# Two feed-forwards in an audio tower: a down projection that runs two inner blocks behind gate and up, and rows that are split into fp16 halves before they are transposed

## Chip, cores, metric

One core of one Trainium2 chip. The metric is the time of one execution on the device in microseconds, the median of several runs. The profile is of one further execution.

## What is computed

Four layers on 4096 rows of 512: an attention-like token mixer, an attention, a feed-forward with ternary weights, an attention with linear bias and a feed-forward with fp4 weights. The change touches the two feed-forwards:

```python
h = h + _L0_ffn_ref(_layernorm(h, axis=-1), L0_ffn_w1, L0_ffn_w3, L0_ffn_w2)
h = h + _L1_attn_ref(_layernorm(h, axis=-1), L1_attn_Wq, L1_attn_Wk, L1_attn_Wv, L1_attn_Wo)
h = h + _L1_ffn_ref(_layernorm(h, axis=-1), L1_ffn_gate_up_packed, L1_ffn_gate_up_scales, L1_ffn_down_packed, L1_ffn_down_scales)
...
g = jax.nn.silu(h1) * h3                                  # first: h1, h3 = x @ ternary w1, w3
return jnp.einsum('bsh,dh->bsd', g, w2q)
...
w_gu = _dequant_fp4(gate_up_packed, gate_up_scales, GROUP_SIZE)   # second: one scale per 128 inputs
h = jax.nn.silu(gate) * up
y = jnp.einsum('bsi,hi->bsh', h, w_down)
rms = jnp.sqrt(jnp.mean(y * y, axis=-1, keepdims=True) + EPS)
return y / rms
```

The inner width is 1365 in the first and 1408 in the second: 11 inner blocks of up to 128.

## The kernel before

The instructions of each engine are written out by hand in the order in which it runs them; semaphores order the engines among each other. Both feed-forwards work in 8 groups of 512 rows, each of 4 tiles of 128 rows. A step `n` runs the 11 inner blocks `m` of group `n`; beside them stand the down projection of group `n-1` and the normalisation of the tiles of group `n+1`, at the blocks in `norm_at` (3, 5, 7, 9).

**Rows.** A tile is normalised on VectorE (`row_stats`, `x_normalised`, with an inverse root on GpSimd between them) into the fp32 tile xn. TensorE transposes xn in four fp32 pieces into the bank px (`transpose_x`, L1728 in the first, L2129 in the second). ScalarE casts px to fp16 (xhi), VectorE subtracts that from px (xlo). The next xn waits for the transposes, the next transposes for xlo. Every product is made with both halves.

**First feed-forward** (`feed_forward`, from L1464). For each inner block TensorE makes 16 matmuls of 512 columns (gate_up, L1717), at blocks 2, 4, 6, 8 also 22 matmuls that project one tile of the group before (finish, L1740), and at 3, 5, 7, 9 a tile's transposes. ScalarE makes silu, VectorE the product prod and glo, ScalarE ghi. In groups 1 to 7 three of five blocks also hold a slot of the decode of the fp4 weights: masks and a join on VectorE (L1394 to L1409), four activations and a cast on ScalarE (L1432 to L1445), two or three products and sums on GpSimd (`pool_value`, L1454 to L1461), loads on SP. GpSimd runs `pool_value` of a block ahead of its inverse root.

**Second feed-forward** (`feed_forward_fp4`, from L1759). As the weights have a scale for each 128 inputs, a block's gate and up are 8 separate sums of two matmuls each (`products_of`, L2119). They go round six banks part0 to part5. ScalarE scales every second one into a tile (`scale_part`, L1922), VectorE scales and adds the ones between (`join_part`, L2006), GpSimd adds the two tiles (`sum_parts`, L1888). The projection of group `n-1` is spread over all 22 half blocks by the table `down_to`, tile after tile, into one bank pz, 33 matmuls each (`project`, L2141); ScalarE copies pz out before the next tile begins (`z_out`, L1954):

```python
down_to = {0: (0, 0, 6), 1: (0, 6, 12), 2: (0, 12, 18), 3: (0, 18, 23), 4: (0, 23, 28), 5: (0, 28, 33),
           6: (1, 0, 7), 7: (1, 7, 14), 8: (1, 14, 21), 9: (1, 21, 27), 10: (1, 27, 33),
```

Then come squares (L1962), mean square (L2054), inverse root (L1875), hout (`output`, L2063) and the store. The last step, `n` = 8, has no gate and up: it projects group 7 alone.

**Between the two** lies the second attention. Its last steps alternate with `normalise(i)` of the second feed-forward's first four tiles, on each engine in its own order (L2160 and on). On VectorE `normalise(i)` is xn, statistics of the next tile, xlo; then the next attention step begins with hout (L837).

## Time and profile before

| | |
|---|---|
| Median of 3 runs | 2389.77 us (2387.38 to 2393.89) |
| Profiled execution, its own time | 2391.57 us |
| Its span | 2389.8 us |
| TensorE busy, share of the span | 2244.2 us, 94% |
| VectorE | 1662.7 us, 70% |
| ScalarE | 1495.3 us, 63% |
| GpSimd | 1021.4 us, 43% |
| Granted TensorE clock | 0.985 |
| Token mixer and first attention | 0 to 957 us |
| First feed-forward, second attention, second feed-forward | 957 to about 1470, to 1801, to 2389.8 us |

Busy time of TensorE is the time in which at least one matmul is under way. Matmuls are pipelined, so a matmul of 512 columns is shown with 0.38 us though the next starts sooner; the distance of starts tells what one costs. Names of tiles stand without their number, f_ is either feed-forward, a_ either attention, fw_ the fp4 decode.

### The profile page before, as it was taken

To read this page: it belongs to the slowest core of one execution; us is meant where nothing else is said; L and a number is where in the kernel's file an instruction comes from. 1 tells how busy PE (TensorE), PEld (TensorE's weight loads), DVE (VectorE), ACT (ScalarE), POOL (GpSimd) and SP (SyncE) were. 2 spreads that over 40 slices of the span, in tenths; PEclk is the share of its full clock that TensorE was granted. 3 is DMA by queue.
4 is the path that set the end of the run, shared out by engine and by line. 5 is a ranking of instruction groups with operands and counts; after the bars stand their busy time and mean duration, and the time that the engine had idled before them with its cause. 6 is when DMAs were issued, how large, how long until landed. Compare 5 with 4: busy or idle time off the path is not lost. (4 is left out here: it accounts for less than half of the span.)

```text
span 2389.8 us, 41107 instructions
## 1 busy us (share of the span) xinstructions
PE 2244.2 (94%) x13188; PEld 1128.5 (47%) x13188; DVE 1662.7 (70%) x2931; ACT 1495.3 (63%) x2398; POOL 1021.4 (43%) x1007
## 2 busy tenths in 40 slices
PE   6999999998999996799999999999987999999998
PEld 2333333335666663344444445666652444444443
DVE  6666666665888887456667634666657888888873
ACT  4666666666788785355656425667745666667663
POOL 1222222237777773223324302444434555555552
PEclk9999999999999998799999999999999999999999
DMA  5545445442343211312223212222221011111101
GB/s 146 138 127 135 129 127 135 130 110 66 111 131 114 67 58 36 109 50 79 80 89 93 67 48 84 80 79 79 79 67 40 23 49 40 53 41 45 45 27 53
DMA packets 144300, 194.94 MB, mean 82 GB/s; under 512 B 32773, under 2 KB 76261, under 8 KB 144154
## 3 DMA queue, kind: packets, MB, share of 16 engines
q1 hardware_dynamic: 115642, 154.79, 21.7%
q10 hardware_dynamic: 28512, 38.28, 5.7%
q8 instruction: 81, 1.33, 0.2%
q14 instruction: 65, 0.53, 0.1%
HBM read 125.10 MB, written 42.21 MB: 70 GB/s over the span
## 5 line engine op out<-in xcount | busy, mean ns | idle before, releaser
L341 DVE TENSOR_REDUCE tm_negmax<-tm_s 128x1 f32<-128x512 f32 x512 | 323.3, 679 | 164.7 <-PE tm_s L384 164.4
L303 ACT ACTIVATE tm_prob<-tm_s 128x1024 f32<-128x1024 f32 x256 | 257.6, 1023 | 136.9 <-PE tm_s L404 130.6
L2119 PE MATMUL f_part<-f_xhi,gu 128*128 128x512 f16 x704 | 269.4, 383 | 17.8 <-ACT f_firstg L1922 6.3
L2119 PE MATMUL f_part<-f_xlo,gu 128*128 128x512 f16 x704 | 268.6, 382 | 0.0
L421 PE MATMUL tm_o<-tm_prob,tm_vt 128*64 128x512 f32 x1024 | 255.7, 620 | 0.0
L1888 POOL TENSOR_TENSOR f_firstg<-f_firstg,f_secondg 128x512 f32<-128x512 f32 x88 | 150.7, 1712 | 193.3 <-DVE f_secondg L2006 193.3
L2141 PE MATMUL f_pz<-dn,f_ghi 128*128 128x512 f16 x704 | 214.5, 380 | 5.9 <-ACT f_zc L1954 5.9
L384 PE MATMUL tm_s<-tm_qk 96*128 96x512 f16 x512 | 199.2, 391 | 14.6 <-DMA tm_qk<-tm_xs 14.1
L264 POOL TENSOR_TENSOR tm_hn<-tm_nd,tm_rows 128x1024 f32<-128x1024 f32 x32 | 75.3, 2353 | 291.8 <-DMA tm_rows<-rden 291.8
L404 PE MATMUL tm_s<-tm_qk 98*128 98x512 f16 x512 | 194.2, 382 | 1.6 <-DMA tm_qk<-tm_mrow 1.6
L975 PE MATMUL a_bankB<-a_wo,a_yThi 128*128 128x512 f16 x512 | 158.7, 393 | 4.1 <-DVE a_yTlo L899 4.0
L1015 PE MATMUL a_bankB<-a_wqkv,a_xhi 128*128 128x512 f16 x512 | 152.9, 380 | 0.3
L1888 POOL TENSOR_TENSOR f_firstu<-f_firstu,f_secondu 128x512 f32<-128x512 f32 x88 | 117.9, 1339 | 70.2 <-DVE f_secondu L2006 69.4
L421 PEld LDWEIGHTS tm_o<-tm_prob,tm_vt 128*64 128x64 f32 x1024 | 92.4, 199 | 112.2 <-issue 85.7
L1740 PE MATMUL f_pz<-tern,f_ghi 128*128 128x512 f16 (+1 forms) x352 | 134.3, 382 | 2.9 <-DVE f_glo L1641 2.9
L1740 PE MATMUL f_pz<-tern,f_glo 128*128 128x512 f16 (+1 forms) x352 | 134.1, 381 | 0.0
L2141 PE MATMUL f_pz<-dn,f_glo 128*128 128x512 f16 x352 | 133.4, 379 | 0.0
L2119 PEld LDWEIGHTS f_part<-f_xhi,gu 128*128 128x128 f16 x704 | 69.1, 98 | 122.4 <-ACT f_firstg L1922 14.1
L384 PEld LDWEIGHTS tm_s<-tm_qk 96*128 96x128 f16 x512 | 50.0, 98 | 155.4 <-issue 86.9
L1456 POOL TENSOR_TENSOR fw_value<-fw_value,fw_code 128x512 f32<-128x512 f32 (+1 forms) x35 | 43.9, 1254 | 185.0 <-DVE fw_value L1409 178.1
L683 ACT COPY a_qT<-a_bankD 128x512 f16<-128x512 f16 x128 | 68.6, 588 | 83.4 <-PE a_bankD L948 83.4
L694 ACT COPY a_kT<-a_bankC 32x512 f16<-32x512 f16 (+1 forms) x192 | 111.1, 578 | 1.5
(190 smaller groups left out, 5668.4 us busy)
## 6 DMA issues: line engine op xcount, KB each, us to landing
tm_qk<-tm_xs SPq DMA_DIRECT2D x384, 64.0 KB, 2.1
tm_xqk<-in_qk ACTq DMA_DIRECT2D x32, 512.0 KB, 4.3
a_hin<-h SPq DMA_DIRECT2D x64, 256.0 KB, 2.7
a_hres<-h SPq DMA_DIRECT2D x64, 256.0 KB, 3.0
h<-a_hout SPq DMA_DIRECT2D x64, 256.0 KB, 2.5
f_hin<-h SPq DMA_DIRECT2D x64, 256.0 KB, 2.7
f_hres<-h SPq DMA_DIRECT2D x64, 256.0 KB, 2.8
tm_vt<-in_vt ACTq DMA_DIRECT2D x32, 256.0 KB, 3.0
```

What stands on the lines that cost most here:

```text
L303: nc.scalar.activation(prob[b][:, 2 * h:2 * h + 2, :], s2[:, i % 2, :, :], ACT.Exp, scale=SCALE).then_inc(exp_done, 1)
L341: nc.vector.tensor_reduce(negmax[u][:, m:m + 1], s1[:, p % BANKS, :], AX.X, ALU.max, negate=True).then_inc(s1_read, 1)
L384: nc.tensor.matmul(s1[:, place(m) % BANKS, :], qk[u][0:KS, 0, b, i * P:(i + 1) * P], qk[u][0:KS, 1, b, :], start=True, stop=True).then_inc ...
L404: last = nc.tensor.matmul(s2[:, i % 2, j, :], qk[u][0:KM, 1, b, s:s + P], qk[u][0:KM, 0, b, :], start=True, stop=True)
L421: last = nc.tensor.matmul(o[2 * C * q:2 * C * (q + 1), :], vt[u][:, j, :, b], prob[b][:, j, :], start=j == 0, stop=j == NT - 1)
L694: last = nc.scalar.copy(kT[rows, :, :, :, j, :].rearrange("p a f b k -> p (a f b) k"), kTp[rows, :].rearrange("p (n k) -> p n k", k=L))
L975: last = nc.tensor.matmul(bankB[:, :], a, w[:, r, :], start=n == 0, stop=n == 3 * R - 1)
L1015: last = nc.tensor.matmul(out, a[u][:, j, :], w[:, j, cols], start=n == 0, stop=n == 3 * KT - 1)
L1740: last = nc.tensor.matmul(pz[i % 2][:, :], gparts[x][u][0:rows[m], m, i * P:(i + 1) * P], down[0:rows[m], m, :], start=c == 0, stop=c == 2 ...
L1888: pool.tensor_tensor(to[:, :], to[:, :], other[:, :], ALU.add).then_inc(s["sum_done"], 1)
L2119: last = nc.tensor.matmul(part[q % BANKS][:, :], (gate, up)[which][:, j, m * P:(m + 1) * P], xparts[x][u][:, j, :], start=x == 0, stop=x == 1)
L2141: last = nc.tensor.matmul(pz[:, :], gparts[x][u][:, m, i * P:(i + 1) * P], down[w][:, m, :], start=c == 0, stop=c == 3 * MT - 1)
```

## The change

**Both feed-forwards.** xn is no longer transposed in fp32. ScalarE casts it to fp16 into halves[:, 0] (`x_high`), GpSimd subtracts that from xn into halves[:, 1] (`x_low`), TensorE transposes both halves in eight fp16 pieces into one bank, and ScalarE copies all 1024 columns to xs (`copy_x`), one block later. VectorE's xlo is gone. The next xn waits for `x_low`, the next split for the transposes, the next transposes for the copy.

**Second feed-forward.** Four banks hold the sums of the four tiles at once, four others take gate and up in turn, with the transposes as one more user of the turn. The projection of block `m-2` runs beside gate and up of block `m`: 12 matmuls, one or two after each pair. The projection of a group so ends two blocks after its gate and up, in the next step. The copies of the sums come in blocks 1 and 2, squares, means and outputs in blocks 3 to 10 of that step. The last step has 24 matmuls. Product and glo of a group's last block moved into block 0 of the next step.

```diff
 def feed_forward(...):
+        def x_low(g, i):
+            if inside(g, GROUPS):
+                t = NT * g + i
+                wait(pool, s["high_done"], t + 1)
+                wait(pool, s["xT_ready"], t)
+                pool.tensor_tensor(halves[:, 1, :], xn[:, :], halves[:, 0, :], ALU.subtract).then_inc(s["low_done"], 1)
...
                 if q is not None:
                     fp4.pool_value(pool, q - 1)
+                if m + 1 in norm_at:
+                    x_low(n + 1, norm_at.index(m + 1))
                 if m + 3 in norm_at:
                     inverse_deviation(n + 1, norm_at.index(m + 3))
...
+        def x_high(g, i):
+            if inside(g, GROUPS):
+                t = NT * g + i
+                wait(act, s["xn_done"], t + 1)
+                wait(act, s["xT_ready"], t)
+                nc.scalar.copy(halves[:, 0, :], xn[:, :]).then_inc(s["high_done"], 1)
+        def copy_x(g, i, u):
             if inside(g, GROUPS):
                 wait(act, s["xT_ready"], NT * g + i + 1)
                 if i == 0:
                     wait(act, s["gu_ready"], MT * (g - 1))
+                nc.scalar.copy(xs[u][:, :, :, i * P:(i + 1) * P].rearrange("p x j n -> p (x j) n"),
+                               px[:, :].rearrange("p (n c) -> p n c", c=P)).then_inc(s["xs_done"], 1)
...
             for m in range(MT):
                 q = slot(n, m)
+                if m - 1 in norm_at:
+                    copy_x(n + 1, norm_at.index(m - 1), 1 - u)
+                if m + 1 in norm_at:
+                    x_high(n + 1, norm_at.index(m + 1))
                 gate_act(n, m, u)
                 if m:
                     hidden_hi(n, m - 1, u)
                 if q is not None:
                     fp4.scalar_high(act, q - 3)
-                if m in norm_at:
-                    x_hi(n + 1, norm_at.index(m), 1 - u)
...
-        def x_lo(g, i, u):
-            if inside(g, GROUPS):
-                wait(dve, s["xhi_done"], NT * g + i + 1)
-                nc.vector.tensor_tensor(xlo[u][:, :, i * P:(i + 1) * P], px[:, :].rearrange("p (j n) -> p j n", j=KT),
-                                        xhi[u][:, :, i * P:(i + 1) * P], ALU.subtract).then_inc(s["xlo_done"], 1)
...
 def feed_forward_fp4(...):
+    turn = [bank[i] for i in (3, 4, 5, 2)]
+    pz = [bank[i] for i in (6, 7, 0, 1)]
...
+    squares_at = [3, 5, 7, 8]
+    mean_at = [4, 6, 8, 9]
+    out_at = [5, 7, 9, 10]
+    LAG = 2
...
+        def step(n):
             for m in range(MT):
+                lagging = (n, m - LAG) if m >= LAG else (n - 1, MT + m - LAG)
                 for which in range(2):
                     for j in range(KT):
-                        products_of(n, m, u, which, j)
-                    project(n - 1, 1 - u, *down_to[2 * m + which])
+                        i = 4 * which + j
+                        products_of(n, m, which, j)
+                        for c in range(3 * i // 2, 3 * (i + 1) // 2):
+                            project(*lagging, c)
                 if m in norm_at:
                     transpose_x(n + 1, norm_at.index(m))
...
 sync:
+            store(n - 1, 0)
             residual(n - 1, 2)
             load(n + 2, 0)
             store(n - 1, 1)
             residual(n - 1, 3)
             load(n + 2, 1)
+            store(n - 1, 2)
+            store(n - 1, 3)
...
 scalar, normalise(i) of the first four tiles:
-            x_hi(0, i, 0)
+            if i:
+                copy_x(0, i - 1, 0)
+            if i < NT:
+                x_high(0, i)
```

GpSimd in group 1 of the first feed-forward, blocks 0 to 5, before (f_rstd is the inverse root, fw_value the two fp4 operations of one chunk):

```order
L1570 TENSOR_TENSOR f_rstd_10644<-f_veps_10642,f_minus_half 128x1
L1456 TENSOR_TENSOR fw_value_10626<-fw_value_10626,fw_code_10622 128x512
L1461 TENSOR_TENSOR fw_value_10626<-fw_value_10626,fw_words_10616 128x512
L1570 TENSOR_TENSOR f_rstd_10645<-f_veps_10643,f_minus_half 128x1
L1456 TENSOR_TENSOR fw_value_10627<-fw_value_10627,fw_code_10623 128x512
L1461 TENSOR_TENSOR fw_value_10627<-fw_value_10627,fw_words_10617 128x512
L1570 TENSOR_TENSOR f_rstd_10644<-f_veps_10642,f_minus_half 128x1
```

The same place of the changed kernel:

```order
L1578 TENSOR_TENSOR f_rstd_10644<-f_veps_10642,f_minus_half 128x1
L1456 TENSOR_TENSOR fw_value_10626<-fw_value_10626,fw_code_10622 128x512
L1461 TENSOR_TENSOR fw_value_10626<-fw_value_10626,fw_words_10616 128x512
L1573 TENSOR_TENSOR f_halves<-f_xn,f_halves 128x512
L1578 TENSOR_TENSOR f_rstd_10645<-f_veps_10643,f_minus_half 128x1
L1456 TENSOR_TENSOR fw_value_10627<-fw_value_10627,fw_code_10623 128x512
L1461 TENSOR_TENSOR fw_value_10627<-fw_value_10627,fw_words_10617 128x512
L1573 TENSOR_TENSOR f_halves<-f_xn,f_halves 128x512
```

The subtraction that the transposes of the next block wait for stands behind the chunk's two fp4 operations.

TensorE at the last gate and up products of the second feed-forward and behind them, before (f_part is a bank of a gate or up sum, f_pz the bank of the down projection; 138 projections follow the last product, 6 of them in its own half block):

```order
L2119 MATMUL f_part<-f_xhi_10730,gu 128x512
L2119 MATMUL f_part<-f_xlo_10732,gu 128x512
L2141 MATMUL f_pz<-dn_10611,f_ghi_10737 128x512
L2141 MATMUL f_pz<-dn_10612,f_ghi_10737 128x512
L2141 MATMUL f_pz<-dn_10611,f_glo_10739 128x512
L2141 MATMUL f_pz<-dn_10611,f_ghi_10737 128x512
L2141 MATMUL f_pz<-dn_10612,f_ghi_10737 128x512
L2141 MATMUL f_pz<-dn_10611,f_glo_10739 128x512
```

The same place of the changed kernel (all banks are named f_bank):

```order
L2171 MATMUL f_bank<-dn_10611,f_ghi_10736 128x512
L2143 MATMUL f_bank<-f_xs_10730,gu 128x512 x2
L2171 MATMUL f_bank<-dn_10612,f_ghi_10736 128x512
L2171 MATMUL f_bank<-dn_10611,f_glo_10738 128x512
L2171 MATMUL f_bank<-dn_10611,f_ghi_10736 128x512
L2171 MATMUL f_bank<-dn_10612,f_ghi_10736 128x512
L2171 MATMUL f_bank<-dn_10611,f_glo_10738 128x512
L2171 MATMUL f_bank<-dn_10611,f_ghi_10736 128x512
```

The projection is mixed among the products, and 26 projections are left behind the last of them.

VectorE where a tile of the second feed-forward is normalised between two steps of the attention, before (a_hout is the attention's output, f_xlo the low half) and in the changed kernel:

```order
L2042 TENSOR_SCALAR f_xn<-f_hin_10715,f_mv_10723,f_rstd_10727 128x512
L2030 BN_STATS f_stats_10720<-f_hin_10714 128x6
L2032 BN_AGGR f_mv_10722<-f_stats_10720 128x2
L2034 TENSOR_SCALAR f_veps_10724<-f_mv_10722 128x1
L2048 TENSOR_TENSOR f_xlo_10731<-f_px,f_xhi_10729 128x4x128
L837 TENSOR_TENSOR a_hout_10675<-a_bankB,a_hres_10673 128x512
```

```order
L2098 TENSOR_SCALAR f_xn<-f_hin_10713,f_mv_10721,f_rstd_10725 128x512
L2086 BN_STATS f_stats_10720<-f_hin_10714 128x6
L2088 BN_AGGR f_mv_10722<-f_stats_10720 128x2
L2090 TENSOR_SCALAR f_veps_10724<-f_mv_10722 128x1
L837 TENSOR_TENSOR a_hout_10675<-a_bankB,a_hres_10673 128x512
```

The operation that waited for TensorE's transposes is gone from ahead of a_hout.

## Rows read from the trace of the kernel before

**Rows 1.** Windows: length, busy PE, PEld, DVE, ACT, POOL (count); clock, DMA, GB/s.

```profile
977.40:1437.00 459.60, 452.71 (x2136) 213.67 (x2136) 274.92 (x464) 230.75 (x382) 130.20 (x114) 0.99 0.24 76
1801.00:1862.00 61.00, 48.76 (x193) 15.73 (x194) 50.46 (x83) 41.25 (x69) 32.76 (x25) 0.97 0.09 27
1862.00:2349.80 487.80, 480.66 (x2247) 219.88 (x2248) 407.10 (x636) 337.91 (x568) 262.43 (x206) 1.00 0.13 41
2349.80:2389.80 40.00, 30.44 (x138) 12.98 (x136) 8.03 (x15) 8.06 (x18) 4.36 (x7) 0.98 0.19 66
```

**Rows 2.** Chain that ended last: start us, us, what.

```profile
2301.74 1.73 PE f_part L2119 x8
```

**Rows 3.** Timeline of PE: transposes in fp32 and in fp16. Start us, us, what.

```profile
1820.99 0.60 PE L2129 MATMUL f_px<-f_ident,f_xn 128*128 128x128 f32 x4
...
1509.48 0.61 PE L948 MATMUL a_bankD<-a_ident,a_qs 128*128 128x128 f16 x8
```

**Rows 4.** Timeline of PE: second feed-forward, first and third inner block.

```profile
1800.96 0.59 PE L2119 MATMUL f_part<-f_xhi,gu 128*128 128x512 f16 x1 [1.49 <-DVE f_xlo L2048]
...
1811.41 0.39 PE L2119 MATMUL f_part<-f_xhi,gu 128*128 128x512 f16 x1 [0.22 <-DVE f_secondg L2006]
```

**Rows 5.** Timelines of ACT and DVE: the last tile.

```profile
2383.08 0.59 ACT L1954 COPY f_zc<-f_pz 128x512 f32<-128x512 f32 x1 [6.63 <-PE f_pz L2141]
2383.70 0.63 ACT L1962 ACTIVATE f_square<-f_zc 128x512 f32<-128x512 f32 x1
...
2385.27 0.75 DVE L2063 SCALAR_TENSOR_TENSOR f_hout<-f_zc,f_rinv,f_hres 128x512 f32<-128x512 f32 x1 [0.66 <-POOL f_rinv L1875]
```

**Rows 6.** DMA issues on the page: KB, us to landing.

```profile
f_hres<-h SPq DMA_DIRECT2D x64, 256.0 KB, 2.8
```

**Rows 7.** Groups by line: busy us, mean ns, idle before.

```profile
L1888 POOL TENSOR_TENSOR f_firstg<-f_firstg,f_secondg 128x512 f32<-128x512 f32 x88 | 150.7, 1712 | 193.3 <-DVE f_secondg L2006 193.3
L2006 DVE SCALAR_TENSOR_TENSOR f_firstg<-f_part,f_factor,f_firstg 128x512 f32<-128x512 f32 x88 | 65.8, 748 | 24.6 <-ACT f_firstg L1922 18.0 <-PE f_part L2119 6.2
L1922 ACT ACTIVATE f_firstg<-f_part,f_factor 128x512 f32<-128x512 f32 x88 | 60.4, 687 | 14.1 <-PE f_part L2119 14.1
```

**Rows 8.** Timelines of PE and DVE: drain of the second attention.

```profile
1774.70 0.60 PE L2129 MATMUL f_px<-f_ident,f_xn 128*128 128x128 f32 x4
...
1775.95 0.69 DVE L2048 TENSOR_TENSOR f_xlo<-f_px,f_xhi 128x512 f16<-128x512 f32 x1 [3.42 <-ACT f_xhi L1945]
1776.56 0.68 DVE L837 TENSOR_TENSOR a_hout<-a_bankB,a_hres 128x512 f32<-128x512 f32 x1
```

**Rows 9.** Timelines of DVE and PE: opening of the first feed-forward.

```profile
965.34 0.55 DVE L1661 TENSOR_SCALAR f_xn<-f_hin,f_mv,f_rstd 128x512 f32<-128x512 f32 x1 [0.73 <-POOL f_rstd L1570]
968.38 0.54 DVE L1661 TENSOR_SCALAR f_xn<-f_hin,f_mv,f_rstd 128x512 f32<-128x512 f32 x1
...
977.44 0.61 PE L1717 MATMUL f_gu0g<-f_xhi,tern 128*128 128x512 f16 x1 [1.40 <-DVE f_xlo L1667]
```

**Rows 10.** Timeline of ACT: 1024 elements out of a bank.

```profile
933.51 1.01 ACT L733 CAST a_pThi<-a_bankS 128x1024 f16<-128x1024 f32 x1 [1.58 <-PE a_bankS L1024]
```

**Rows 11.** Timelines of POOL, PE, ACT, DVE: two tiles of the first feed-forward.

```profile
1036.24 1.26 POOL L1461 TENSOR_TENSOR fw_value<-fw_value,fw_words 128x512 f32<-128x512 f32 x1
...
1038.42 0.60 PE L1728 MATMUL f_px<-f_ident,f_xn 128*128 128x128 f32 x4
...
1333.85 0.68 ACT L1590 ACTIVATE f_act_out<-f_gu0g,tern_scales 128x512 f32<-128x512 f32 x1
...
1337.74 0.54 DVE L1661 TENSOR_SCALAR f_xn<-f_hin,f_mv,f_rstd 128x512 f32<-128x512 f32 x1
...
1342.97 1.54 POOL L1461 TENSOR_TENSOR fw_value<-fw_value,fw_words 128x512 f32<-128x512 f32 x1
...
1339.92 0.60 PE L1728 MATMUL f_px<-f_ident,f_xn 128*128 128x128 f32 x4
```

**Rows 12.** Groups by line: gate products of odd blocks.

```profile
L1717 PE MATMUL f_gu1g<-f_xhi,tern 128*128 128x512 f16 (+1 forms) x176 | 66.7, 379 | 2.9 <-DVE f_xlo L1667 2.9
```

More of the change, by code:

```diff
@@ L2055, in mean_square, with output @@
                     .then_inc(s["ms_done"], 1)
-        def output(g, i, half):
+        def output(g, i):
             if inside(g, GROUPS):
@@ L2087, in step, with products_of @@
+                join_part(n, m, 1, 3)
+                if m in out_at:
+                    output(n - 1, out_at.index(m))
                 if m + 3 in norm_at:
-                    i = norm_at.index(m + 3)
-                    row_stats(n + 1, i, 2 * (n + 1) + i // 2)
-            hidden(n, MT - 1, u)
-            hidden_lo(n, MT - 1, u)
+                    row_stats(n + 1, norm_at.index(m + 3))
         return normalise, begin, step
     def tensor(pe):
+        def products_of(g, m, which, j):
+            if inside(g, GROUPS):
+                i = 4 * which + j
+                if m == 0 and i == 0:
+                    wait(pe, s["xs_done"], NT * (g + 1))
+                wait_bank(pe, g, m, i)
+                for x in range(2):
+                    last = nc.tensor.matmul(bank_of(m, i)[:, :], (gate, up)[which][:, j, m * P:(m + 1) * P],
+                                            xs[g % 2][:, x, j, :], start=x == 0, stop=x == 1)
+                last.then_inc(s["part_ready"], 1)
@@ new lines, in transpose_x @@
+        def transpose_x(g, i):
+            if inside(g, GROUPS):
+                t = NT * g + i
+                px = (bank_of(None, i) if g else turn[3])[:, :].bitcast(F16)
+                wait(pe, s["low_done"], t + 1)
+                if g:
+                    wait_bank(pe, g - 1, None, i)
+                else:
+                    wait(pe, s["xs_done"], t)
+                for x in range(2):
+                    for j in range(KT):
+                        last = nc.tensor.transpose(px[:, (x * KT + j) * P:(x * KT + j + 1) * P],
+                                                   halves[:, x, j * P:(j + 1) * P], ident[:, :])
+                last.then_inc(s["xT_ready"], 1)
@@ new lines, in project @@
+        def project(g, m, c):
+            if inside(g, GROUPS):
+                i, (x, w) = c // 3, products[c % 3]
+                if c == 0:
+                    wait(pe, s["glo_done"], MT * g + m + 1)
+                if m == 0 and c % 3 == 0:
+                    wait(pe, *(pz_free[i] if g == 0 else (s["zc_done"], NT * (g - 1) + i + 1)))
+                last = nc.tensor.matmul(pz[i][:, :], gparts[x][g % 2][:, m, i * P:(i + 1) * P], down[w][:, m, :],
+                                        start=m == 0 and c % 3 == 0, stop=m == MT - 1 and c % 3 == 2)
+                if m == MT - 1 and c % 3 == 2:
+                    last.then_inc(s["z_ready"], 1)
@@ L2100, in begin @@
         def begin():
-            for n in ("qT_copied", "pTlo_done", "y_done", "yTlo_done"):
+            for n in ("qT_copied", "pTlo_done"):
                 pe.wait_ge(*before.done[n])
-        def sums_begin():
-            pe.wait_ge(*before.done["out_done"])
-        def products_of(g, m, u, which, j):
-            if inside(g, GROUPS):
-                i = 4 * which + j
-                q = 8 * m + i
-                if q == 0:
-                    wait(pe, s["xlo_done"], NT * (g + 1))
-                used = 8 * MT * g + q - BANKS if q >= BANKS else 8 * MT * (g - 1) + (84 if q < 4 else 78) + q
-                if q >= BANKS or not isinstance(g, int) or g:
-                    wait(pe, s[("scale_done", "join_done")[j % 2]], used // 2 + 1)
-                for x in range(2):
-                    last = nc.tensor.matmul(part[q % BANKS][:, :], (gate, up)[which][:, j, m * P:(m + 1) * P],
-                                            xparts[x][u][:, j, :], start=x == 0, stop=x == 1)
-                last.then_inc(s["part_ready"], 1)
@@ L2195, in _ @@
         att.all_rows(sp)
-        run(step_u, 0, 9)
+        for n in range(9):
+            step_u(n)
         unit_rows(sp)
@@ L2219, in _ @@
             normalise(i)
-        run(step_u, 0, 9)
+        for n in range(9):
+            step_u(n)
     @block.scalar
@@ L2247, in _ @@
                 run(step, 31 + i, 31 + i)
-        run(step_u, 0, 9)
+        normalise(4)
+        for n in range(9):
+            step_u(n)
     @block.vector
@@ L2273, in _ @@
         begin()
-        run(step_u, 0, 9)
+        for n in range(9):
+            step_u(n)
     @block.tensor
@@ L2295, in _ @@
         begin()
-        run(step_u, 0, 0)
-        sums_begin()
-        run(step_u, 1, 9)
+        for n in range(9):
+            step_u(n)
 def three_bf16(a):
```

290 lines of the change are left out of this document (138 added, 152 removed), and 3 rows, old and new, of the table down_to.

## The prediction

> **What bounds the kernel now.** I read the page's busy shares first and then the busy time in windows [rows 1]. In the first feed-forward TensorE is busy for 452.7 of 459.6 us, in groups 1 to 7 of the second for 480.7 of 487.8 us. Two stretches of the second are different: its group 0 (61.0 us, 48.8 busy) has nothing to project yet, and in the last 40.0 us there is only projection left. So TensorE's stream of matmuls sets the time nearly everywhere, and whatever makes it wait is paid in full. The yardstick is the chain of waits [rows 2]: eight 512-column matmuls start within 1.73 us, 0.216 us each.
>
> **Transposes.** Four fp32 ones take 0.60 us from the first start to the last end, eight fp16 ones 0.61 us [rows 3]. TensorE wins nothing from halves: cost 0 for all 64 tiles, and the change must live from the order of work.
>
> **Second feed-forward, groups 1 to 7.** 7 x (176 + 132) matmuls x 0.216 = 465.7 us, and six sets of four tiles' transposes at 0.43 us (0.60 less the 0.17 us by which a matmul outlasts its turn) = 10.3 us: 476.0 us if nothing waits, against 487.8 and the 1.3 us of six projections of the last block that ran behind the window's end, 489.1. The waits that go are those of the single sum pz (it had to be copied out between two tiles) and of the burst at a group's end. Can four banks carry it? An inner block is now 28 matmuls, 6.05 us; a bank comes round after four pairs and their share of projection, 3.0 us. ScalarE has per block four scalings and some copies, VectorE four joins (means 0.69 and 0.75 us [rows 7]) and two passes of the hidden values: about 3.9 us each, and up to 5.9 us where norms and outputs fall too. Laid end to end on the 6.05 us, the bank needed soonest is free 1.0 us early or more. I take -13.1 us; bounds 0 (as many waits as before) and -14 us.
>
> **Group 0.** The third inner block started 10.4 us after the first [rows 4]. With four banks instead of six to fill ahead I take 11.4. From there the projection of block 0 runs along: 9 x 6.05 + 4 x 0.43 = 56.2. Group 0 takes 67.6 instead of 61.0: +6.6 us (bounds +5 to +9).
>
> **The end.** After the last block there were 132 matmuls and the chain of the last tile, 38.7 us (40.0 less those 1.3). Now there are 24 matmuls. The last glo needs one sum on GpSimd, the product, ghi and glo: ready about 3.9 us after the last products, so TensorE waits 1.4 us and ends at 6.6. The four tiles are then ready together, and their chains queue: four copies at 0.59 on ScalarE, four squares at 0.8 with the read of their sums [rows 5], so output 1 is done at 10.6. The third and fourth output need residuals that SP loads only after outputs 0 and 1, 2.8 us to landing [rows 6]: output 3 starts at 13.9. From the last hout's start to the end of the span it was 4.5 us [rows 5]. That makes 18.4 us where it was 38.7: -20.3 us (bounds -17 and -22).
>
> **Attention's drain.** VectorE stood at xlo, which needs the transposes, and those were queued behind 12 matmuls of the output projection; only after xlo came hout and the next tile's work [rows 8]: hout started 1776.56, while its own bank was complete about 1775.0. xlo is gone, so hout moves up 1.6 us in two rounds: -3.2. The last tile's chain is longer (ScalarE split, GpSimd subtraction, 1.01 us copy [rows 10] instead of 0.59 + 0.69), but its normalisation starts earlier: about 0. Bounds 0 and -3.3. Second feed-forward in all: -13.1 + 6.6 - 20.3 - 3.2 = **-30.0 us**.
>
> **First feed-forward, the opening.** Before, one tile took 3.0 us (xn 965.34, 968.38) and the first product started at 977.44 [rows 9]. Now a tile's ring is split on ScalarE 0.6, subtraction on GpSimd 1.3, transposes 1.1 at the low clock, copy of 1024 elements 1.0 [rows 10], since one pair of halves and one bank serve all: 4.1 us. +5.0 us for four tiles (4 to 6).
>
> **First feed-forward, the tiles on the way.** This is the largest unknown. GpSimd runs the fp4 decode; the new subtraction stands behind the two fp4 sums of its inner block, and those wait for a VectorE join that itself comes after this block's product. TensorE reaches the transposes 38 matmuls, 8.2 us, after the gate and up sums of that block. Laying 1.27 us (an fp4 product takes 1.26 and 1.54 in [rows 11]) plus 0.1 us behind GpSimd's end for each of the 28 tiles of groups 0 to 6, 17 are in time and 11 are late, by 16.2 us in sum. The first late one: GpSimd free at 1037.5, subtraction to 1038.9, transposes had started 1038.42. The worst: GpSimd free at 1344.5, transposes at 1339.92 [rows 11]. A second pass counts what the new ScalarE work adds ahead of silu (it must now wait for xn, and where the decode ran just before, the copy of the previous tile stands there too): in group 6 silu ran at 1333.85, xn ends 1338.28, so product, join and fp4 sums all move by 1.5 us, and that tile is 7.5 us late. Eight others move by 0.6 to 1.7 us; waits already paid take some away. I get **22.5 us**. Bounds: 10 (half absorbed by later slack) and 28. Two of these waits are over 3.5 us. After the drain and its last wait of 1.49 us [rows 4], group 0 of the second part ran at a granted clock of 0.97 over 61 us [rows 1], 1.8 us lost; two of that: +3.6 (0 to 7).
>
> **First feed-forward, group borders.** At three borders TensorE waited 2.9 us for xlo (f_gu1g [rows 12]; two more at f_gu0g). Now the copy of the last tile stands behind four decode steps of ScalarE in the same block: 1.5 us more, three times, +4.5 (2 to 6). All: 5.0 + 22.5 + 3.6 + 4.5 = **+35.6 us**.
>
> Hidden and costed at nothing: split and 1.01 us copy in the second part (ScalarE was busy 338 of 488 us, the change adds some 4 us a group), x_low there (GpSimd 262 of 488), xlo's removal from VectorE (407 of 488). If that cover were gone, 0.5 us a tile, 14 us.
>
> **The sum.** 2391.57 us is the profiled execution's own time. 2391.6 - 30.0 + 35.6 = 2397.2. That execution lies 1.8 us above the median of 2389.77, so the forecast for the median is **2395 us**: two large terms of opposite sign that nearly cancel. A measurement of this kernel can tell about 0.3% (7 us) from no change, so this is "the same", at its upper edge.
>
> **Rivals.**
> - *The late tiles of the first part are absorbed* (0.25). For it: 17 of 28 tiles had 0.3 to 5.5 us of slack, and every wait of TensorE gives the other engines time to catch up, also at the borders. Against: the chain starts from the same gate and up sums each time, so a wait doesn't shorten the next one. If only the opening and 8 us are left, 2389.8 - 30 + 13 = 2373 us.
> - *Four banks are too few* (0.10): slower, the other side. If one bank in each inner block comes free 0.35 us late (a join behind a late hout would do it), TensorE loses 0.35 x 77 = 27 us and the time is 2422 us. It decides once VectorE or ScalarE needs more than about 1 us above what I laid end to end. The six banks of before still waited in the first blocks of a group, and so it isn't excluded.
> - *The subtraction on GpSimd is longer* (0.20). The same form on GpSimd takes 1.26 us at its shortest [rows 11] but 1.71 in the mean beside VectorE's joins [rows 7]. With 1.75 in place of 1.27, 11 to 14 tiles are 0.5 us later, and VectorE operations held up move joins too: 7 to 13 us more, 2405 us. The Trainium skill (SBUF — State Buffer, "Who interferes with whom") says that a VectorE instruction with two SBUF inputs and a GpSimd instruction that reads SBUF exclude each other for a whole instruction; the 1.71 beside 1.27 agrees, and by that rule this rival is the likelier of the two slower ones.
> - That the change doesn't do what it says I leave out: the order on TensorE shows two gate and up products between projections of one block down to the end.
>
> **Numbers.** Forecast 0.45 with a range of its own of 2387 to 2403: 0.03 faster, 0.32 within 0.3%, 0.10 slower. Absorbed 0.25: 0.22 and 0.03. Four banks 0.10: slower. Longer subtraction 0.20: 0.05 within and 0.15 slower. Together: faster 0.25, same 0.40, slower 0.35. The range that leaves out 2 in 10 reaches into the first rival below and past the third above: 2372 to 2413 us.
>
> **What would show it.** Right, if group 0 of the second part lasts 66 to 69 us, each later group 68 to 68.5, and the stretch after the last gate product 17 to 20; if TensorE waits for the new GpSimd subtraction some 15 to 25 us between the first and last transposes of the first part, the longest in its group 6; and if the first gate product comes about 5 us later. Wrong, if gate and up products wait for scalings or joins in every block (four banks), or if the first part is longer by under 15 us.

## The result, and the profile after

The changed kernel takes **2400.31 us** (median of 9 runs, 2396.65 to 2402.76); the kernel before, timed beside it, 2391.58 us (9 runs, 2386.39 to 2395.74). The ratio is 1.0035, 95% interval 1.0023 to 1.0046: 8.7 us slower, clear of no change; the 0.3% (7 us) that the forecast took as the edge of "the same" lies inside the interval, so on which side of that edge the kernel stands isn't settled (a chance of 0.35 stood on slower, 0.40 on the same). The time is inside the range of 2372 to 2413 us. The profiled execution took 2401.46 us with a span of 2399.7 us. All times below are medians, and each stands beside the kernel before as timed with it on the same chip; of the run `residuals_early` one of four executions (3632 us, at a clock of 0.60) was disturbed and isn't used.

First, the busy time in windows of the changed kernel, cut at the same events as in [rows 1]: first feed-forward, group 0 and groups 1 to 7 of the second, and what follows the last gate and up product (length, then busy PE, PEld, DVE, ACT, POOL with counts; clock, DMA share, GB/s).

```profile
985.80:1478.10 492.30, 462.53 (x2248) 215.47 (x2248) 269.90 (x436) 258.59 (x410) 161.71 (x142) 0.97 0.22 71
1836.40:1903.60 67.20, 65.64 (x316) 29.40 (x317) 50.25 (x80) 47.90 (x74) 37.69 (x29) 0.97 0.08 24
1903.60:2379.30 475.70, 475.70 (x2348) 221.54 (x2347) 376.75 (x613) 359.02 (x594) 295.63 (x230) 1.00 0.13 42
2379.30:2399.70 20.40, 5.89 (x27) 2.31 (x25) 6.15 (x12) 6.48 (x15) 3.94 (x6) 0.75 0.34 116
```

In groups 1 to 7 TensorE is now busy without a gap: 475.70 of 475.70 us. The first feed-forward grew from 459.6 to 492.3 us, and of the 32.7 us more only 9.8 are busy time.

TensorE's waits in the first feed-forward, by what ended them (engine, line, releaser: us in total, times, longest):

```profile
PE f_px L1740 <- POOL f_halves L1573: 19.9, 7, 7.4
PE f_gu1g L1728 <- ACT f_xs L1622: 5.3, 2, 2.7
PE f_gu0g L1728 <- DVE f_prod L1653: 3.0, 3, 1.5
PE f_gu0g L1728 <- ACT f_xs L1622: 2.4, 2, 1.3
```

The first row is new: seven sets of transposes wait for GpSimd's subtraction. Counted from start to start it is 21.4 us, since a matmul's shown end lies 0.17 us behind its turn and an eighth wait of 0.3 us is too short for the list. The worst of them on GpSimd's timeline (start us, us, what, idle time and releaser) ...

```profile
1375.20 1.27 POOL L1456 TENSOR_TENSOR fw_value<-fw_value,fw_code 128x512 f32<-128x512 f32 x1 [5.63 <-DVE fw_value L1409]
1376.61 1.53 POOL L1461 TENSOR_TENSOR fw_value<-fw_value,fw_words 128x512 f32<-128x512 f32 x1
1378.11 1.60 POOL L1573 TENSOR_TENSOR f_halves<-f_xn,f_halves 128x512 f16<-128x512 f32 x1
```

... and what TensorE, ScalarE and VectorE did meanwhile:

```profile
1370.49 1.89 PE L1728 MATMUL f_gu1u<-f_xs,tern 128*128 128x512 f16 x8
1379.77 1.04 PE L1740 MATMUL f_px<-f_ident,f_halves 128*128 128x128 f16 x8 [7.39 <-POOL f_halves L1573]
...
1370.60 0.62 ACT L1615 CAST f_halves<-f_xn 128x512 f16<-128x512 f32 x1 [4.53 <-DVE f_xn L1680]
1371.12 0.68 ACT L1600 ACTIVATE f_act_out<-f_gu0g,tern_scales 128x512 f32<-128x512 f32 x1
...
1374.44 0.68 DVE L1409 TENSOR_TENSOR fw_value<-fw_value,fw_bend 128x512 f32<-128x512 f32 x1
```

The high half was there at 1371.2. GpSimd stood still for 5.63 us before the fp4 sum, waiting for VectorE's join (ready at 1375.1), while the subtraction behind it had all it needed. The join was late for the same kind of reason one engine further on: on ScalarE the silu of the next product (1371.12) now stands behind the cast, and the cast waited 4.53 us for xn. Against the moment at which TensorE came to its transposes, the join ended 2.9 us late here (1375.1 against 1372.2) and 1.5 us late at the same tile before (1341.5 against 1339.9 [rows 11]), as VectorE's row there shows:

```profile
1340.78 0.68 DVE L1409 TENSOR_TENSOR fw_value<-fw_value,fw_bend 128x512 f32<-128x512 f32 x1
```

What remains after the last gate and up product, on VectorE, TensorE, GpSimd, ScalarE and SP's queue, to compare with [rows 5, 6]:

```profile
2379.59 0.75 DVE L2062 SCALAR_TENSOR_TENSOR f_secondu<-f_bank,f_factor,f_secondu 128x512 f32<-128x512 f32 x1 [0.64 <-ACT f_secondu L1970]
2380.42 1.71 POOL L1934 TENSOR_TENSOR f_firstu<-f_firstu,f_secondu 128x512 f32<-128x512 f32 x1 [1.05 <-DVE f_secondu L2062]
...
2383.59 0.69 DVE L2078 TENSOR_TENSOR f_glo<-f_prod,f_ghi 128x512 f16<-128x512 f32 x1 [0.68 <-ACT f_ghi L1986]
2384.34 0.60 PE L2171 MATMUL f_bank<-dn,f_ghi 128*128 128x512 f16 x2 [1.91 <-DVE f_glo L2078]
2385.20 2.53 ACT L2010 COPY f_zc<-f_bank 128x512 f32<-128x512 f32 x4 [1.64 <-PE f_bank L2171]
2387.62 0.63 ACT L2018 ACTIVATE f_square<-f_zc 128x512 f32<-128x512 f32 x1
...
2391.84 0.43 SPq L1860 DMA_DIRECT2D f_hres<-h  x1
2395.13 0.75 DVE L2113 SCALAR_TENSOR_TENSOR f_hout<-f_zc,f_rinv,f_hres 128x512 f32<-128x512 f32 x1 [1.02 <-DMA f_hres<-h]
```

The glo that TensorE waits for is ready at 2384.3, 5.3 us after the last product started (2379.0), and before the last output VectorE idles 1.02 us for a residual that was issued at 2391.84.

### The profile page after: what moved, and what is told of

Same layout as the page of the kernel before. It is cut to its first block and busy times, and to the rows that moved or that the text cites. A ratio compares the mean times of both kernels' runs of the same rounds, so it can differ in the third digit from the quotient of the medians.

```text
span 2399.7 us, 41805 instructions
## 1 busy us (share of the span) xinstructions
PE 2241.7 (93%) x13444; PEld 1136.8 (47%) x13444; DVE 1621.3 (68%) x2867; ACT 1557.2 (65%) x2462; POOL 1100.0 (46%) x1071
## 5 line engine op out<-in xcount | busy, mean ns | idle before, releaser
L2143 PE MATMUL f_bank<-f_xs,gu 128*128 128x512 f16 x1408 | 418.6, 380 | 2.8 <-ACT f_xs L2001 1.2
L2171 PE MATMUL f_bank<-dn,f_ghi 128*128 128x512 f16 x704 | 265.5, 379 | 1.9 <-DVE f_glo L2078 1.9
L2143 PEld LDWEIGHTS f_bank<-f_xs,gu 128*128 128x128 f16 x1408 | 136.4, 98 | 164.9 <-issue 3.7
L1934 POOL TENSOR_TENSOR f_firstu<-f_firstu,f_secondu 128x512 f32<-128x512 f32 x88 | 124.0, 1409 | 65.0 <-DVE f_secondu L2062 65.0
L2171 PE MATMUL f_bank<-dn,f_glo 128*128 128x512 f16 x352 | 133.4, 379 | 0.0
L635 POOL TENSOR_TENSOR a_qs<-a_qkv,a_qs 128x512 f16<-128x512 f32 x32 | 37.1, 1159 | 173.7 <-ACT a_qs L752 173.7
L611 POOL TENSOR_TENSOR a_crossed<-a_qkv,a_sin 128x64 f32<-128x64 f32 (+1 forms) x128 | 81.7, 657 | 76.4 <-ACT a_qkv L722 76.3
```

Source lines behind the costliest of these rows:

```text
L611: pool.tensor_tensor(dst[:, :, :, e], src[:, :, :, 1 - e], sin[:, e, :].unsqueeze(1).broadcast_to([P, n, 8]), ALU.mult).then_inc(s["crosse ...
L1934: pool.tensor_tensor(to[:, :], to[:, :], other[:, :], ALU.add).then_inc(s["sum_done"], 1)
L2143: last = nc.tensor.matmul(bank_of(m, i)[:, :], (gate, up)[which][:, j, m * P:(m + 1) * P], xs[g % 2][:, x, j, :], start=x == 0, stop=x == 1)
L2171: last = nc.tensor.matmul(pz[i][:, :], gparts[x][g % 2][:, m, i * P:(i + 1) * P], down[w][:, m, :], start=m == 0 and c % 3 == 0, stop=m == ...
```

## Experiments

**Each part alone.** `second_only` is the changed kernel with the first feed-forward of before, whole, and a second, fp16 identity beside the fp32 one; `first_only` the reverse. Beside the exchanged function the edit is this:

```diff
+    ident16 = sb("ident16", [P, P], F16)
+        sp.dma_start(ident16[:, :], const["ident16"]).then_inc(c_in, 16)
```

> Only the second feed-forward is changed; the first keeps fp32 transposes and the old xhi/xlo. Theory (the terms are independent and each as it stands in the trace of the change: attention's stretch -5.8 us, groups of the second part -5.8, end -19.7): 31 us less than before, 2360 us (2355 to 2365). Rival A (the two parts are coupled: part of the second part's gain is time that was only shifted there by the later start of its inputs): 2365 to 2375. Also looked at: in the changed kernel TensorE had a half-clock stretch at 562 to 580 us, in code that neither part touches, worth 4 us; if it came from where code or tiles lie, this kernel shows it too, if it is chance, it may not.

> Only the first feed-forward is changed; the second keeps the old order and the old xhi/xlo. Theory (opening 4.2 us, waits for halves at the transposes 21.4, borders 3.0, clock after the waits 6 to 9): 35 to 38 us more than before, about 2427 us. Rival (the waits are partly absorbed by attention behind it, where the stretch became 5.8 us shorter in the changed kernel): 2415 to 2422 us.

Measured: second part alone 2364.15 us against 2394.93, ratio 0.9877 [0.986, 0.9893], **-30.8 us**; first part alone 2432.26 against the same, 1.0163 [1.0146, 1.018], **+37.3 us**. The sum, +6.5, is within 2.2 us of what both together cost (+8.7), less than the intervals of some 4 us can tell from nothing. The stages say it more sharply: groups 1 to 7 of the second part last 475.4 us with either first part. No interaction is seen, and rival A of the first and the rival of the second fall. From first to last gate and up product the first feed-forward lasts 491.7 us in `first_only` and 492.3 in the changed kernel, 459.4 in `second_only` and before.

**The subtraction ahead of the fp4 sums.** In the changed kernel, first part:

```diff
+                if m + 1 in norm_at:
+                    x_low(n + 1, norm_at.index(m + 1))
                 if q is not None:
                     fp4.pool_value(pool, q - 1)
-                if m + 1 in norm_at:
-                    x_low(n + 1, norm_at.index(m + 1))
```

> The changed kernel, with the GpSimd subtraction of the first part ahead of the fp4 sums of its inner block instead of behind them. Theory (the transposes wait only because the subtraction stands behind the fp4 sums, and the half-clock stretches come from those waits): the 21.4 us of waits fall under 3, the stretches at half clock inside groups 1 to 6 of the first part go, 26 to 30 us less than the changed kernel: 2370 to 2374 us. Rival A (the split on ScalarE, which waits for xn, is late itself): waits of 8 to 12 us stay, 2382 to 2388. Rival B (the fp4 sums move 1.2 us later and ScalarE's or VectorE's decode steps with them, so silu and the product are late): TensorE waits for the product instead, gate and up sums start late by 0.5 to 1 us in 28 blocks, 2385 to 2400.

Measured: 2375.96 us against 2394.93, ratio 0.9926 [0.991, 0.9943]. That is 19.0 us less than before, where the changed kernel takes 8.7 more: 27.7 us between them, though the bare medians, from two sets of runs, lie 24 apart, and 2376 is 2 us above the 2370 to 2374 that theory gave. The stage says it more exactly: 465.3 us instead of 492.3. TensorE's waits there:

```profile
PE f_gu1g L1728 <- ACT f_xs L1622: 5.3, 2, 2.7
PE f_gu0g L1728 <- DVE f_prod L1653: 3.0, 3, 1.5
PE f_gu0g L1728 <- ACT f_xs L1622: 2.4, 2, 1.3
```

Three rows are the changed kernel's to the tenth, and the fourth, 19.9 us for POOL, is gone. Both rivals fall: the high half isn't late, and the decode takes the 1.2 us without making a product late. One thing of the theory didn't come: the half-clock stretches behind the two waits of 2.7 us for f_xs stayed. 27.0 us went where 21.4 were waits. The other 5.6 are the clock, as the changed kernel's windows around one wait show (columns as above, clock third from the end):

```profile
1324.00:1331.00 7.00, 4.20 (x20) 1.69 (x18) 5.81 (x11) 5.62 (x10) 3.24 (x3) 1.00 0.41 131
1331.40:1338.00 6.60, 5.28 (x19) 2.50 (x20) 2.28 (x3) 1.53 (x2) 2.89 (x3) 0.50 0.31 99
1338.40:1345.00 6.60, 6.60 (x32) 3.02 (x31) 3.85 (x6) 4.42 (x7) 1.47 (x1) 1.00 0.01 2
```

```profile
1326.31 1.89 PE L1728 MATMUL f_gu0u<-f_xs,tern 128*128 128x512 f16 x8
1332.72 1.04 PE L1740 MATMUL f_px<-f_ident,f_halves 128*128 128x128 f16 x8 [4.52 <-POOL f_halves L1573]
1333.55 3.62 PE L1728 MATMUL f_gu1g<-f_xs,tern 128*128 128x512 f16 x8
```

TensorE stood still for 4.5 us, the granted clock fell to 0.50 (1.2 of 2.4 GHz), and the next eight gate matmuls took 3.62 us instead of 1.89.

**The copy back in its old place as well.** On top of that:

```diff
-                if m - 1 in norm_at:
-                    copy_x(n + 1, norm_at.index(m - 1), 1 - u)
                 ...
                     fp4.scalar_high(act, q - 3)
+                if m in norm_at:
+                    copy_x(n + 1, norm_at.index(m), 1 - u)
```

> As the run with the subtraction ahead, and ScalarE's copy of the transposed halves (first part) is back in the inner block of its transposes, ahead of the decode preparation, where xhi stood. Theory: the wait at each group's first gate product (1.4 to 2.9 us, seven borders) falls under 1 us: 3 to 8 us less than with the subtraction alone, 2364 to 2370 us. Rival (the copy waits for the transposes and holds back the decode and the next block's silu): no gain or up to 10 us more, 2372 to 2382.

Measured: 2367.14 us against 2394.93, ratio 0.9885 [0.9867, 0.9903]. The stage lasts 457.9 us, now below the 459.4 of before: waits for f_xs at a group's first product 1.1 us instead of 7.7, and no stretch at half clock is left between the opening and the end of the stage. One late subtraction (1.4 us) came back, and waits for prod grew from 3.0 to 4.4 us. The theory holds: gain 7.4 us in the stage, where it asked for 3 to 8.

**What carries the second part's gain?** Two halves of the change, each without the other, in a kernel whose first part is as before. `order_only`: lag of two, four sums, four banks, but fp32 transposes with xhi and xlo taken from the bank (the edit below, abridged, against the changed kernel). `halves_only`: the old order (one sum, six banks, a bank of its own for the transposes) with the split rows.

```diff
-                nc.scalar.copy(halves[:, 0, :], xn[:, :]).then_inc(s["high_done"], 1)
-                pool.tensor_tensor(halves[:, 1, :], xn[:, :], halves[:, 0, :], ALU.subtract)...
+                nc.scalar.copy(xs[u][:, 0, :, i * P:(i + 1) * P], px.rearrange(...)).then_inc(s["high_done"], 1)
+                nc.vector.tensor_tensor(xs[u][:, 1, :, i * P:(i + 1) * P], px.rearrange(...),
+                                        xs[u][:, 0, :, i * P:(i + 1) * P], ALU.subtract).then_inc(s["xs_done"], 1)
```

> Only the second feed-forward is changed, and of it only the order of work: down projection two blocks behind, four sums, four banks in turn; the rows are transposed as fp32 and split by ScalarE and VectorE from PSUM as before (xhi, xlo). Theory (the order carries the gain of groups and end, the halves ahead of the transposes give only attention's drain, 3.6 us in the run with the second part alone): attention's stretch back at 364, groups at 68 to 69, end 20.5: 2366 to 2370 us. Rival (the bank of a tile's transposes now comes free only after xhi and xlo stood in two queues, and one of only four banks is held that long): TensorE waits 0.5 to 1 us at each of 28 tiles, groups at 70 to 72, 2382 to 2396 us.

> Only the second feed-forward is changed, and of it only the rows: split into halves ahead of fp16 transposes, copied once; the order of the projection, the single sum and the six banks stay. The second part's groups lasted 70.0 us before, 69.6 with the new order alone, 68.3 with both. Theory (the halves help the groups only where a transposed tile occupies one of the four banks in turn; here it has a bank of its own): attention's stretch 3.6 us shorter, groups 69.9 to 70.1, 2389 to 2391 us where before has 2393 to 2395. Rival (the halves relieve VectorE of 0.7 us a tile in any order, and this is what let the groups go to 68.3): groups 68.7 to 69.3, 2381 to 2386 us.

Measured: order alone 2378.18 us against 2393.47, 0.9934 [0.9917, 0.995], between theory and rival; halves alone 2397.0 against 2391.42, 1.0023 [1.0011, 1.0035], outside both: slower than before. One of groups 1 to 6 of the second part lasts, in the median (first gate product to first gate product):

| | old rows | split rows |
|---|---|---|
| old order | 70.0 us | 70.8 us |
| new order | 69.6 us | 68.3 us |

Neither half does much for a group; together they take 1.7 us. For the whole kernel the order does more: alone it takes 15.3 us, mainly because the end shrinks from 40.4 to 20.8 us with it, while the halves alone cost 5.6 us and both together take 30.8. So the order carries the end, and the gain inside the groups needs both. TensorE's waits point to the reason. Order alone, groups 1 to 7:

```profile
PE f_bank L2118 <- DVE f_xs L2071: 5.3, 12, 0.4
```

```profile
1897.84 0.55 DVE L2064 TENSOR_SCALAR f_xn<-f_hin,f_mv,f_rstd 128x512 f32<-128x512 f32 x1 [1.56 <-PE f_bank L2132]
1898.30 0.74 DVE L2028 SCALAR_TENSOR_TENSOR f_secondu<-f_bank,f_factor,f_secondu 128x512 f32<-128x512 f32 x1
1898.96 0.68 DVE L2071 TENSOR_TENSOR f_xs<-f_bank,f_xs 128x512 f16<-128x512 f32 x1
```

and halves alone (a fifth row, 1.3 us, stands the same in before):

```profile
PE f_pz L2160 <- ACT f_zc L1979: 5.3, 7, 0.9
PE f_part L2136 <- ACT f_firstg L1940: 3.1, 7, 0.8
PE f_part L2136 <- DVE f_firstu L2031: 2.5, 7, 0.4
PE f_part L2136 <- DVE f_firstg L2031: 1.8, 7, 0.3
```

The largest wait of the kernel before in these groups:

```profile
PE f_pz L2141 <- ACT f_zc L1954: 3.1, 7, 0.5
```

With four banks in turn, the bank that holds a tile's transposes is needed again soon, and xlo (f_xs L2071) on VectorE sets it free last: in the rows above the next xn waits 1.56 us for the transposes, and behind it stand the join f_secondu, to 1899.0, and xlo, to 1899.6. The split ahead of the transposes ends that use with one copy on ScalarE. In the old order, the split gives ScalarE a cast and a copy of 1024 columns where there was one cast (busy 351 of 492 us in that window, 338 of 488 before), and the wait for the single sum pz grows to 0.9 us at its longest from 0.5. In `second_only` the profile lists no wait of TensorE in that stretch. That xlo's place in the queue is the cause for the order alone, and ScalarE's longer work for the halves alone, is read from these rows; no run moves either by itself.

**The end.** `second_only` with four residual buffers, all four loads at the start of SP's step:

```diff
-    hres = pair("hres", [P, DM], F32)
+    hres = pair("hres", [P, DM], F32) + [extra_sb(f"hres{i}", [P, DM], F32) for i in (2, 3)]
             residual(n - 1, 1)
+            residual(n - 1, 2)
+            residual(n - 1, 3)
```

> The run with the second part alone (2364.2 us), with four residual buffers and SyncE loading all four residuals of a group at the start of its step. Theory (outputs 2 and 3 at the end wait for residuals that are asked for only after outputs 0 and 1, 3.1 us to landing, and the last output's rinv was done 2.4 us before it started): the stretch after the last gate and up product falls from 20.5 to about 18 us, 2361 to 2362 us, where the forecast had put it with the wait (18.4). Rival (the outputs are bound by the squares on ScalarE and the stores anyway): 20 us, 2364.

Measured: three executions of 2356.77, 2358.76 and 2366.12 us, against 2393.47. The stretch fell from 20.5 to 19.1 us, a little over half of what theory gave; the median's further gain over `second_only` is scatter, as the 9 us between its executions say. The residuals' wait is gone, and another took its place: the last output waits for a store of the second, because only two output buffers are there.

```profile
2350.46 0.75 DVE L2104 SCALAR_TENSOR_TENSOR f_hout<-f_zc,f_rinv,f_hres 128x512 f32<-128x512 f32 x1 [0.68 <-DMA out<-f_hout]
```

**The opening, and all together.** `opening_two_banks` lets the transposes of the run `low_copy_ahead` go to two banks in turn and, before the first group, splits tile i+1 before it copies tile i. `best_new` adds the early residuals.

```diff
-    px = ps("px", [P, 2 * KT * P], F16)
-    ps("free", [P, DM], F32)
+    px = [ps(f"px{i}", [P, 2 * KT * P], F16) for i in range(2)]
```

> The run with subtraction and copy ahead (2367.1 us, both parts changed), with the transposed halves going to two banks in turn and, before the first group, ScalarE splitting tile i+1 before it copies tile i. Theory (a tile's ring at the opening is split 0.6, subtraction 1.15, transposes 1.1 and copy 0.9, 3.9 us in all; the copy leaves the ring): 2.5 to 3 us less to the first gate product, 2364 us. Rival (the loads of the rows or the statistics bind the opening): 0 to 1 us less, 2366 to 2367.

> All three together: both parts changed, subtraction and copy ahead, opening through two banks, four residual buffers in the second part. If the gains add: 2367.1 less 2.8 and 2.5, 2361 to 2363 us, about 32 us less than before and 38 less than the changed kernel. If the opening gives nothing, 2364 to 2365.

Measured: 2366.18 us against 2393.47, 0.9888 [0.9872, 0.9905], and 2360.57 against the same, **0.987 [0.9852, 0.9887]**. From the first xn to the first gate product it is 12.1 us in all six profiles with the old first part, 16.3 or 16.4 in the five with the changed one, 13.8 in the three with two banks: the 2.5 us are there, though the medians don't show them: 27.3 us less than before, where `low_copy_ahead` had 27.8 less (the paragraph on chance bears on that). `best_new` beats both kernels, by 33 and by some 40 us, and came 0.4 us below the 2361 to 2363 that the sum of the gains gave.

**The end once more.** Four output buffers too, and in the last step ScalarE squares each tile right after its copy:

```diff
+            if n == GROUPS:
+                hidden_hi(n - 1, MT - 1)
+                for i in range(NT):
+                    z_out(n - 1, i)
+                    squares(n - 1, i)
+                return
```

> The best run so far (2360.6 us), with four output buffers as well and, at the end of the last group, ScalarE squaring each tile right after its copy instead of after all four copies. Theory (with early residuals the stretch after the last gate and up product was 19.1 us: the first square waits for four copies, 1.8 us, and the fourth output waited 0.7 us for a store of the second): outputs start 1.0 to 1.8 us earlier, the stretch is 17.5 to 18.1 us, the time 2359 to 2360. Rival (the squares end no earlier, since ScalarE's sum of work is the same, and GpSimd's powers follow them): 18.6 to 19.1 us.

Measured: the stretch is 17.1 us, a little better than theory; the time 2363.74 us (2357.80 to 2364.12) against 2393.69, ratio 0.9865 [0.9847, 0.9883], above the 2359 to 2360 of theory and not to be told from `best_new`. The two profiles say where the 2 us went: in this one the first xn came 4.8 us later and attention's stretch lasted 1.6 us longer, both ahead of the place that was edited. Which of the two edits gave the gain isn't told apart.

**Chance in code that nobody changed.** The changed kernel's first xn came 4.1 us later than before, though token mixer and first attention are the same instructions. Both kernels were profiled again as they are.

> The kernel before, as it is, profiled a second time. In ten profiles the first gate product of the first feed-forward came at two places, some 4 us apart, among kernels with the same opening, and those with the later one had a longer half-clock stretch at 562 us in code that no kernel changed. Theory (chance of one execution): this profile may show either; if it shows the stretch, its first gate product comes at about 981.5 us. Rival (it belongs to the kernels in which the first part or the tiles' places differ): no such stretch, 977.4 us; this one run can't settle for the rival.

> The changed kernel, as it is, profiled a second time. Theory (chance): if the half-clock stretches at 562 to 580 us are missing, the first gate product comes at about 982 us instead of 985.8 and the rest of the stages are the same to 0.5 us, 2396 us. Rival (systematic): 985.8 again, 2400 us.

Measured: the kernel before 2388.50 us, the changed kernel 2402.45, where chance would have had 2396; first xn at 965.3 and 965.9 us in the two profiles of before, at 969.5 and 967.3 in those of the changed kernel. That alone would speak for the rival. But over all 14 profiles six lie at 965.0 to 965.9 and eight at 967.3 to 970.2, and each kind of kernel is in both: `second_only` at 965.5, `order_only` with the same first part at 969.8; `low_ahead` at 965.6, `low_copy_ahead` at 969.4. The clock differs there: in this window its mean is 1.00 in four profiles, which are all early, 0.74 to 0.77 in five, which are all late, and 0.91 in five of both sorts. Window 560 to 580 us, kernel before and changed kernel:

```profile
560.00:580.00 20.00, 13.90 (x139) 9.71 (x136) 13.98 (x23) 15.47 (x28) 18.07 (x24) 1.00 0.27 82
```

```profile
560.00:580.00 20.00, 14.24 (x118) 10.01 (x116) 10.53 (x18) 11.70 (x21) 15.77 (x23) 0.75 0.22 66
```

`halves_only`, with the old first part, reads 0.74 at the same place. So a single execution carries some 4 us of luck, as large as several terms of the sum. Stages carry luck too, where the clock falls inside them: attention's stretch lasted 364.1 and 360.0 us in the two profiles of before, the first feed-forward 492.3 and 494.3 in the two of the changed kernel (its half-clock stretch behind the longest wait was 10.2 us long instead of 6.8). Groups 1 to 7 of the second part, at a clock of 1.00, repeat to 0.1 us: 487.4 twice, and 475.4 in nine profiles. Of 34 more executions of before, timed beside the other runs, the five at a mean clock of 0.986 took 2387.5 to 2391.0 us and the fourteen at 0.982 or 0.983 took 2393.4 to 2396.6. So the kernel before loses clock in some executions as well; in which stage, no trace says. What starts the half-clock stretch in one execution and not in another stays open, and since neither profile of the changed kernel is without it and neither of before has it, that a kernel's build tilts the odds isn't excluded.

## Why the prediction was right

The forecast, two large terms that nearly cancel and a time at the upper edge of "the same", is what came: -30.8 and +37.3 us measured apart, -30.0 and +35.6 predicted. That both sums came so close is in part luck: the clock cost 5 us more than forecast and groups 1 to 7 with the end 1.7 us more, while attention's stretch, borders, late tiles and opening cost 0.8 to 2.6 us less each. Of the 5.3 us between 2395 and 2400.3, 1.8 are the yardstick (nine runs of before gave 2391.6, not 2389.8).

| term | predicted | measured |
|---|---|---|
| second part, group 0 | +6.6 | +6.2 |
| groups 1 to 7 and the end | -33.4 | -31.7 |
| attention's stretch | -3.2 | -5.8 in this pair of profiles |
| opening | +5.0 | +4.2 |
| late tiles | +22.5 | +21.4 |
| clock behind them | +3.6 | about +8.7 |
| group borders | +4.5 | +3 |

The right column adds up to +6.0 us, the left to +5.6; with the 4.1 us by which the first xn came later (chance by the paragraph above, as far as it goes) it is +10.1, and the two spans differ by 9.9.

*Group 0 and groups 1 to 7.* 67.2 and 475.7 us, where the forecast had 67.6 and 476.0. The laid-out slack of "1.0 us early or more" was enough, and the rival of too few banks has nothing for it here: no listed wait. It isn't far, though: with xlo back in VectorE's queue (`order_only`) twelve waits of some 0.4 us for a bank are listed.

*The step that failed* is the first: "the change must live from the order of work", halves costed at 0. TensorE indeed gains nothing from fp16 transposes (0.61 us for a tile, as before), and the order does carry the end. But with the order alone groups 1 to 7 of the second part last 483.2 us, 4.2 less than before, and with both 475.4, 12.0 less: 7.8 of these 12.0 us need the halves, where the prediction gave all of its 13.1 to the order. The sum came out because the banks had been laid out with no xlo on VectorE; whoever had followed the explanation and kept the old rows would have had 15.3 us less than before instead of 30.8.

*The end.* It took 20.4 us instead of 18.4. Two sizes were off: glo was ready 5.3 us after the last product started instead of 3.9, since VectorE's last join waited 0.64 us for ScalarE and the sum took 1.71 us; and the last residual took 3.2 us to land, not 2.8.

*Attention's drain.* The stretch lasted 364.1, 360.0, 364.1 and 364.6 us in the four profiles with the old rows in the second part, 356.6 to 360.8 (mean 359.2) in ten with the split: 4.0 us on average against 3.2, with a spread of as much. Where xlo stood, from the start of attention's third last output to the first gate product, the two kinds don't overlap: 23.3 to 26.3 us with the old rows, 21.6 to 22.7 with the split, 1.8 us between the medians. So a gain is there; whether all of the 3.2 is, the scatter of the rest hides.

*The late tiles.* Mechanism, place and size held: seven waits by the profile where eleven had been laid out, the longest 7.5 us in group 6 as forecast. So the rival of absorption falls. So does the longer subtraction: it took 1.157 us in the median, less than the 1.27 assumed. Only two of 32 reached 1.60, the one at 1378.11 and the one at 1331.07, each beginning 0.14 us after a VectorE subtraction with both inputs in SBUF (f_glo). The Trainium skill (SBUF — State Buffer, "Who interferes with whom") has these two exclude each other for a whole instruction. Both rows agree roughly: 0.44 us longer, where f_glo still had 0.6 us to run. They stand before the two longest waits, so this was worth 0.9 of the 21.4 us. With the subtraction moved ahead none of 32 is longer (1.150 to 1.166 us); where a f_glo began after one, at 1100.85, it was f_glo that took 1.23 us instead of 0.68.

*The clock.* Named, but mis-sized: two waits over 3.5 us were counted, a limit that no row of before gave. The clock fell behind three waits for the subtraction (2.9, 4.7 and 7.5 us), 5.6 us lost in all, and behind the two border waits of 2.8 us, 3.1 us: after the one that ended at 1283.67 the first eight gate matmuls took 3.48 us instead of 1.89; after the one at 1155.89 the fall came 1.3 us later. Waits of 1.3 to 2.4 us brought no fall.

*The borders.* Two of three waits grew by 1.2 to 1.5 us as predicted, the third by 0.3.

## What to carry to other kernels

An operation put behind a waiting one on a shared in-order engine inherits that wait: here one exchanged pair of lines on GpSimd was worth 27 us, so lay out not only how long each instruction takes but what stands ahead of it. A change of order and a change of operand form can be worth little apart (0.4 and -0.8 us a group) and 1.7 together, so time the kernel with neither, each and both before crediting one. When two large terms cancel, split the kernel first: the half that gains is a better kernel than either, here by 31 us than before and by 36 to 39 than the changed kernel.

## What the runs showed of the hardware

The granted clock of a stretch no kernel touched differed from one execution to the next (1.00, 0.91 or about 0.75 over 560 to 580 us); the first xn behind it came 3.3 to 4.9 us later in the five profiles at about 0.75 than in the four at 1.00. And a wait of TensorE can cost more than its length: 1.6 us extra for the wait of 2.8 us that ended at 1283.67, since the next eight matmuls ran at 1.2 GHz, and nothing extra for those of 1.3 to 2.4 us. Beside a GpSimd multiplication of 1.15 us at 1380.19, VectorE's normalisation, which reads one SBUF tile, took more than twice its usual 0.54 us; in the changed kernel's first feed-forward twelve of these took 1.12 us or more, each beside an operation on GpSimd:

```profile
1380.19 1.15 POOL L1454 TENSOR_TENSOR fw_words<-fw_words,fw_scale 128x512 f32<-128x512 f32 x1
```

```profile
1380.25 1.37 DVE L1680 TENSOR_SCALAR f_xn<-f_hin,f_mv,f_rstd 128x512 f32<-128x512 f32 x1 [0.90 <-POOL f_rstd L1578]
```
